# Projections of two gated cross-attention layers as three float32r products

## The reference, cut to what matters

```python
def layer(x, ctx, attend, ffn, g):        # two layers, B=4, S=512, D=256, 16 heads of 16
    x = x + tanh(g_xattn) * attend(norm(x), ctx, ctx)
    return x + tanh(g_ffn) * ffn(norm(x))
# layer 0: Q = x@Wq.T + bq, K = ctx@Wk.T + bk, V = ctx@Wv.T + bv
#          softmax(Q K / 4 - 0.1*|i-j|) V, then @Wo.T + bo; FFN with ternary weights (256-1024-256, relu)
# layer 1: relu(x@Wq.T), relu(ctx@Wk.T), relu(ctx@Wv.T), softmax attention without bias
#          FFN with 4 experts, argmax routing (256-1024-256, gelu), then a layer norm of its own
```

## Time and profile before

| | us |
|---|---|
| median of 3 runs (766.58 to 767.68) | 766.68 |
| the profiled execution | 764.96 |
| its span | 763.1 |

### The profile page before, as it was taken

One profiled execution on the slowest core, in us unless ns is written; L12 is line 12 of the kernel. 1 busy time (PEld: TensorE's weight loads), 2 busy tenths in 40 slices (PEclk: granted clock), 3 DMA queues, 4 the chain that ended last, 5 costly groups with the idle time before them and its releaser, 6 DMA issues.

```text
span 763.1 us, 12507 instructions
## 1 busy us (share of the span) xinstructions
PE 702.1 (92%) x4252; PEld 424.1 (56%) x4252; DVE 565.4 (74%) x1054; ACT 451.5 (59%) x968; POOL 340.8 (45%) x409
## 2 busy tenths in 40 slices
PE   6878999999998898899998999999999699999993
PEld 3444444444443566597763444444444488989983
DVE  5565899999992369455887999999996656765663
ACT  2322788888888443765414888888887234333330
POOL 3213455555555232763520021645653555755542
PEclk9999999999999999999999999999999889999998
DMA  7788645554554514102144255422201222211000
GB/s 222 214 263 187 200 144 182 180 188 144 182 191 170 166 55 114 40 1 78 37 123 112 79 180 177 140 85 84 76 3 74 85 109 78 78 36 51 27 15 15
DMA packets 51421, 87.53 MB, mean 115 GB/s; under 512 B 8661, under 2 KB 16855, under 8 KB 51360
## 3 DMA queue, kind: packets, MB, share of 16 engines
q1 hardware_dynamic: 43184, 71.39, 29.7%
q0 software_dynamic: 4640, 11.54, 5.1%
q10 hardware_dynamic: 3536, 3.81, 1.7%
HBM read 44.92 MB, written 41.63 MB: 113 GB/s over the span
## 4 chain that ended last, share of the span: by engine, by line
PE 58%; DVE 13%; POOL 12%; issue 8%; DMA 4%; SPq 3%; ACT 2%; POOLq 0%; DVEq 0%; ACTq 0%
PE ps_out L811 9%; PE ps_out L1029 6%; PE ps_wide L1004 6%; PE ps_wide L680 6%; PE ps_a L794 6%; PE ps_a L596 4%; PE ps_misc L794 3%; PE ps_a L929 3%; POOL w_lo L1312 3%; SPq L495 2%; PE ps_a L1018 2%; DVE rows_all L1559 2%; PE ps_out L943 2%; PE ps_wide L607 1%; DMA rows_all<-in_x 1%
## 5 line engine op out<-in xcount | busy, mean ns | idle before, releaser
L1593 DVE TENSOR_REDUCE row_max<-ps_wide 128x2 f32<-128x1024 f32 x256 | 301.9, 1220 | 20.4 <-PE ps_wide L680 19.6
L1142 ACT ACTIVATE probs<-ps_a 128x512 f32<-128x512 f32 (+1 forms) x418 | 199.1, 522 | 28.3 <-PE ps_a L794 27.7
L680 PE MATMUL ps_wide<-stack_k,stack_q 48*128 48x512 f32 x512 | 145.1, 469 | 7.9 <-DVE row_max L1593 3.9
L794 PE MATMUL ps_a<-stack_q,stack_k 62*128 62x512 f32 (+3 forms) x418 | 137.5, 391 | 2.9 <-ACT probs L1142 1.9
L811 PE MATMUL ps_out<-probs,vals 128*17 128x512 f32 x1024 | 134.1, 598 | 0.5 <-POOL probs L1372 0.5
L1142 ACT ACTIVATE probs<-ps_misc 128x512 f32<-128x512 f32 (+1 forms) x222 | 114.0, 514 | 16.4 <-PE ps_misc L794 13.8
L1372 POOL TENSOR_TENSOR probs<-probs,fixes_sb 128x512 f32<-128x512 f32 x64 | 82.2, 1285 | 90.3 <-ACT probs L1142 90.3
L794 PEld LDWEIGHTS ps_a<-stack_q,stack_k 62*128 62x128 f32 (+1 forms) x418 | 63.6, 184 | 68.3 <-ACT probs L1142 31.5
L680 PEld LDWEIGHTS ps_wide<-stack_k,stack_q 48*128 48x128 f32 x512 | 68.3, 184 | 46.9 <-DVE row_max L1593 27.0
L794 PE MATMUL ps_misc<-stack_q,stack_k 62*128 62x512 f32 (+3 forms) x222 | 87.7, 395 | 1.3 <-ACT probs L1142 1.3
L794 PEld LDWEIGHTS ps_misc<-stack_q,stack_k 62*128 62x128 f32 (+1 forms) x222 | 40.9, 184 | 39.1 <-ACT probs L1142 30.4
(11 more groups left out here) (246 smaller groups left out, 1341.1 us busy)
## 6 DMA issues: line engine op xcount, KB each, us to landing
rows_sorted<-blank SPq DMA_DIRECT2D x17, 1040.0 KB, 5.0
planes_k<-planes SPq DMA_DIRECT2D x32, 256.0 KB, 3.7
stack_k<-planes_k SPq DMA_DIRECT2D x64, 128.0 KB, 2.8
planes_q<-planes SPq DMA_DIRECT2D x32, 256.0 KB, 3.6
stack_q<-planes_q SPq DMA_DIRECT2D x64, 128.0 KB, 2.8
w_raw<-in_L_W SPq DMA_DIRECT2D x6, 1024.0 KB, 5.8
stack_k<-planes_k SPq DMA_DIRECT2D x64, 64.0 KB, 2.5
stack_q<-planes_q SPq DMA_DIRECT2D x64, 64.0 KB, 2.7
```

Of the source, the lines that this page charges most:

```text
L680: mm(raw_slot(l, ("pair", g, p))[:, i * S:(i + 1) * S], stack_q[at, slot(g, c) + q * P:slot(g, c) + (q + 1) * P], stack_k[at, slot(g, c):s ...
L794: mm(score_slot(("tile", n))[:, start:end], stack_k[at, slot(g, c) + k * P:slot(g, c) + (k + 1) * P], stack_q[at, slot(g, c) + start:slot( ...
L1142: do(probs[n % PROBS[l]][:, j, start:end], score_slot(("tile", n * TILES + t))[:, start:end], ACT.Exp, scale=0.25).then_inc(exp_done, 1)
L1593: v.tensor_reduce(row_max[:, g % 2, :, p], raw_slot(l, ("pair", g, p))[:].rearrange("p (i k) -> p i k", i=2), AX, ALU.max).then_inc(sem(f" ...
```

## The change

Keys, values and queries of both layers are made as three products of float32r parts (high by high, low weights by high rows, high weights by low rows) instead of float32 matmuls: six matmuls a unit, twelve a values step. The context is split once into `ctx_hi` and `ctx_lo` and used by both layers: batch 0 by ScalarE (high) and VectorE (low), batches 1 to 3 by GpSimd (`context_split(b + 1)` behind `keys_low(0, b)`). Layer 0's weights are split by VectorE (w_k, and every low part) and ScalarE (high parts of w_v and w_q); layer 1's by GpSimd (`weights_split`: w_k at group 4 of layer 0's attention, w_v behind that attention, w_q behind layer 1's keys). Turned rows get a high part from ScalarE's copy and a low part from VectorE (`rows_low0`, `rows_low2`), for which queries and the reuse of the banks now wait. `xT` is gone; the attention's output goes to `att_rows`. ScalarE runs one small copy at the very start. In the experts' stage `prepare(3)` moves ahead of the roots of blocks 0 and 1, and `finish` scales the rows before it waits for the root. Several semaphores are shared between the two layers (counts go on from l * G); those lines are left out.

```diff
+                ctx_lo = sb("ctx_lo", [P, C, B * S], F32R, inputs_)
+            turned_x = sb("turned_x", [P, 2, C, S], F32R, pro)
...
+                att_rows = sb("att_rows", [P, 2, C, S], F32, s0)
+                sb("gap_stacks", [P, 2 * RING * S], F32, s0)
+                w_v_hi1 = sb("w_v_hi1", [P, C, D], F32R, s0)
...
+                x_parts = [sb(f"x_{h}", [P, 2, C, S], F32R, s1) for h in PARTS]
+                w_v_hi0 = sb("w_v_hi0", [P, C, D], F32R, s1)
+                w_q_hi0 = sb("w_q_hi0", [P, C, D], F32R, s1)
...
+        def context_parts(b):
+            return ctx_hi[:, :, b * S:(b + 1) * S], ctx_lo[:, :, b * S:(b + 1) * S]
+
+        def rows_parts(b):
+            return [part_[:, b % 2] for part_ in x_parts]
+
+        def weight_parts(l, s_):
+            hi = {(0, "k"): w_k_hi, (0, "v"): w_v_hi0, (0, "q"): w_q_hi0, (1, "k"): w_k_hi, (1, "v"): w_v_hi1, (1, "q"): w_k_hi}[l, s_]
+            return hi[:], w_lo[s_][:]
 
         def turned_of(b):
-            return turned_x[:, b % 2]
+            return turned_x[:, 0], turned_x[:, 1]
...
-                for k in range(C):
-                    last = mm(proj_bank(l, s_, b, c), w_qkv[s_][:, k, c * P:(c + 1) * P],
-                              src(b)[:, k], start=(k == 0), stop=(k == C - 1))
+                weights, rows = weight_parts(l, s_), src(b)
+                for i, (r, w) in enumerate(PRODUCTS):
+                    if i == 0 and (l, s_, b) == (0, "k", 0):
+                        pe.wait_ge(sem("parts_high"), C)
+                        pe.wait_ge(sem("parts_low"), 2)
+                    if i == 2 and (l, s_, b) == (0, "k", 0):
+                        pe.wait_ge(sem("parts_low"), 2 + C)
+                    if i == 0 and (l, s_, b) == (0, "q", 0):
+                        pe.wait_ge(sem("parts_low"), C + 4)
+                    if i == 2 and (l, s_) == (0, "q"):
+                        pe.wait_ge(sem("x_low"), C * (b + 1))
+                    if i == 0 and l == 0 and s_ == "k" and b > 0:
+                        pe.wait_ge(sem("ctx_low"), C * b)
+                    if i == 0 and (l, s_, b) == (1, "q", 0):
+                        pe.wait_ge(sem("ctx_low"), C * (B - 1) + 3)
+                    if (l, s_) == (1, "q") and i == (0 if b == 0 else 2):
+                        pe.wait_ge(sem("x_low"), C * (B + b + 1))
+                    if i == 0 and (l, s_, b) == (1, "k", 0):
+                        pe.wait_ge(sem("ctx_low"), C * (B - 1) + 1)
+                    for k in range(C):
+                        last = mm(proj_bank(l, s_, b, c), weights[w][:, k, c * P:(c + 1) * P], rows[r][:, k],
+                                  start=(i == 0 and k == 0), stop=(i == 2 and k == C - 1))
                 last.then_inc(made(l, s_, "proj_done", b, c)[0], 1)
...
+                if v == 0 and l == 0:
+                    pe.wait_ge(sem("parts_low"), C + 3)
+                elif v == 0:
+                    pe.wait_ge(sem("ctx_low"), C * (B - 1) + 2)
+                weights, rows = weight_parts(l, "v"), context_parts(v // 2)
                 for i in range(2):
-                    t = 2 * v + i
-                    for k in range(C):
-                        last = mm(vals_bank(l, v)[:, i * D:(i + 1) * D], ctxT[:, k, t * P:(t + 1) * P], w_qkv["v"][:, k, :],
-                                  start=(k == 0), stop=(k == C - 1))
+                    at = slice((2 * v + i) % QT * P, ((2 * v + i) % QT + 1) * P)
+                    for n, (r, w) in enumerate(PRODUCTS):
+                        for k in range(C):
+                            last = mm(vals_bank(l, v)[:, i * D:(i + 1) * D], rows[r][:, k, at], weights[w][:, k, :],
+                                      start=(n == 0 and k == 0), stop=(n == 2 and k == C - 1))
...
-                        pe.wait_ge(sem("turned_read_n2"), (b - 1) * C + c + 1)
+                        pe.wait_ge(sem("x_low"), (B + b - 1) * C + c + 1)
...
-                    wait(pe, sem("turned_read_n0"), (b - 1) * C + i + 1)
+                    wait(pe, sem("x_low"), (b - 1) * C + i + 1)
...
-                        last = mm((po, pm)[t % 2][:, 0:D], xT[:, k, t * P:(t + 1) * P], w_o[:, k, :],
+                        last = mm((po, pm)[t % 2][:, 0:D], att_rows[:, b % 2, k, t % QT * P:(t % QT + 1) * P], w_o[:, k, :],
...
+                    if name == "n0":
+                        do(x_parts[0][:, b % 2, c, :], spare_banks[c][:], ACT.Copy).then_inc(sem("turned_read_n0"), 1)
+                    else:
+                        do(att_rows[:, b % 2, c, :], wide(u), ACT.Copy).then_inc(sem("turned_read_att"), 1)
...
+            act.wait_ge(sem("half_ready"), 1)
+            do(quant[:, 0:1], minus_half[:, 0:1], ACT.Copy)
...
+            for c in range(C):
+                do(ctx_hi[:, c, 0:S], context_of(0)[:, c, :], ACT.Copy).then_inc(sem("parts_high"), 1)
...
+                    if b == 0:
+                        act.wait_ge(loaded_values, 16 * N_VALUES)
+                        do((w_v_hi0, w_q_hi0)[c][:], w_qkv["vq"[c]][:], ACT.Copy).then_inc(sem("parts_high"), 1)
...
+            def context_split(b):
+
+                pool.wait_ge(sem(f"loaded_in{b}"), 16 * N_IN)
+                for c in range(C):
+                    hi, lo, raw = (z[:, c, b * S:(b + 1) * S] for z in (ctx_hi, ctx_lo, ctxT))
+                    v.tensor_copy(hi, raw).then_inc(sem("ctx_high"), 1)
+                    pool.wait_ge(sem("ctx_high"), C * (b - 1) + c + 1)
+                    v.tensor_tensor(lo, raw, hi.bitcast(F32), ALU.subtract).then_inc(sem("ctx_low"), 1)
...
+            def weights_split(s_):
+
+                n = C * (B - 1) + "kvq".index(s_) + 1
+                (hi, lo), raw = weight_parts(1, s_), w_qkv[s_][:]
+                pool.wait_ge(sem("w_layer1"), 16 * 3)
+                v.tensor_copy(hi, raw).then_inc(sem("ctx_high"), 1)
+                pool.wait_ge(sem("ctx_high"), n)
+                v.tensor_tensor(lo, raw, hi.bitcast(F32), ALU.subtract).then_inc(sem("ctx_low"), 1)
...
+                    if l == 0 and g == QT:
+                        weights_split("k")
...
                 keys_low(0, b)
+                if b + 1 < B:
+                    context_split(b + 1)
...
             attention(0)
+            weights_split("v")
             for b in range(B):
                 keys_low(1, b)
                 roots(1, b)
+            weights_split("q")
...
                 gather(FIRST + n)
+            prepare(3)
             for n in range(2):
                 root4(n)
             for n in range(2):
                 scatter(n)
             for n in range(2, BLOCKS):
                 root4(n)
-                if n + 1 < BLOCKS:
+                if 2 < n < BLOCKS - 1:
                     prepare(n + 1)
...
+            def weight_low(s_):
+
+                hi, lo = weight_parts(0, s_)
+                v.tensor_tensor(lo, w_qkv[s_][:], hi.bitcast(F32), ALU.subtract).then_inc(sem("parts_low"), 1)
+
+            def rows_low0(b):
+
+                for c in range(C):
+                    dve.wait_ge(sem("turned_read_n0"), b * C + c + 1)
+                    v.tensor_tensor(x_parts[1][:, b % 2, c, :], spare_banks[c][:], x_parts[0][:, b % 2, c, :].bitcast(F32), ALU.subtract
+                                    ).then_inc(sem("x_low"), 1)
+
+            v.tensor_copy(w_k_hi[:], w_qkv["k"][:]).then_inc(sem("parts_low"), 1)
+            dve.wait_ge(sem("parts_low"), 1)
+            weight_low("k")
+            for c in range(C):
+                dve.wait_ge(sem("parts_high"), c + 1)
+                v.tensor_tensor(context_parts(0)[1][:, c, :], context_of(0)[:, c, :], ctx_hi[:, c, 0:S].bitcast(F32), ALU.subtract
+                                ).then_inc(sem("parts_low"), 1)
             dve.wait_ge(loaded_rows, 16 * N_ROWS)
             variance(0, 0, x, 1e-5)
+            dve.wait_ge(loaded_values, 16 * N_VALUES)
+            dve.wait_ge(sem("parts_high"), C + 1)
+            weight_low("v")
             normal(0, 0, x)
-            dve.wait_ge(loaded_values, 16 * N_VALUES)
+            dve.wait_ge(sem("parts_high"), C + 2)
+            weight_low("q")
             for b in range(B):
                 for c in range(C):
                     first_maxima(0, *FIRST_RAWS.get((b, "k", c), (0, 0)))
                 for i in range(2):
                     values0(2 * b + i)
                     first_maxima(0, *FIRST_RAWS.get((b, "v", i), (0, 0)))
+                rows_low0(b)
...
                 if b == B - 1:
-                    dve.wait_ge(sem("turned_read_n0"), B * C)
+                    dve.wait_ge(sem("x_low"), B * C)
...
+            def rows_low2(b):
+
+                for c in range(C):
+                    dve.wait_ge(sem("turned_read_n2"), b * C + c + 1)
+                    v.tensor_tensor(turned_x[:, 1, c], n2_bank(b, c), turned_x[:, 0, c].bitcast(F32), ALU.subtract
+                                    ).then_inc(sem("x_low"), 1)
...
                     if q == 1 and b == 1:
+                        rows_low2(0)
```

(11 more changed lines are left out.)

58 lines of the change are left out of this document (31 added, 27 removed).

## The result

The changed kernel takes 773.64 us (median of 5, 770.57 to 775.74) against 766.58 us (763.51 to 767.68) for the kernel before: a ratio of 1.0103, 95% interval 1.0078 to 1.0128. It is slower, by 7 to 8 us where the forecast had 2.3 and a range up to 772.5. The profiled execution is the fastest of its five, 770.57 us with a span of 768.2; against the profiled one of before (763.1) it is 5.1 us longer.

The account below looks back on a forecast made before the run. TensorE holds 58% of the chain but does not end the first stage, where VectorE and GpSimd do. First stage +5.7, third -1.9 and experts -1.5 sum to +2.3 us: forecast 769.0 us, range 762.5 to 772.5.

Parts of the forecast that it names:

- The signs that the forecast named: Batch 1 keys near 29.5, attention 5.7 us later, clock fall before 50, shorter third stage, `turned_x` low wait, no 1.8 wait.
- The saving on TensorE: Projections: 0.32 us saved per key or query unit, 0.31 per values step; 15.2 us in all, as a ceiling.
- The head: First stage, first batch: splitting and GpSimd beside VectorE delay keys of batch 1 by 6.6 us, to 29.5; low end 2.7.
- Rival 1: Head is cheaper: first batch loses only 2.7 us, batch 1 keys at 25.6, total 763.7 us; chance 0.27.
- Batches 1 to 3: First stage after the head: +0.5, -0.8 and -2.0 us for batches 1, 2 and 3.
- The clock: First stage: of two 3.7 us TensorE pauses, one is followed by a clock fall costing about 1.4 us.
- the third (771.4): Rival: clock falls twice in the first stage and again beside the wait of query batch 1; 771.4 us, chance 0.13.
- Layer 0's attention: The w_k split on GpSimd, 1.9 us once, is covered by idle time: 0; without cover 1.9 us.
- Third stage, keys and values: Layer 1's keys and values save 5.1 us, less 1.3 where VectorE is last and 0.6 for GpSimd: -3.2 us.
- Third stage, the rest: Layer 1's queries wait for low parts, +1.3 us in sum; whole third stage -1.9 us, bounds -4.5 and +0.5.
- Experts: Last stage: moving `prepare(3)` and scaling earlier gives 1.1 us, last block's scaling 0.4; -1.5 us, bounds -0.4 and -2.2.

Follow-up runs that it names:

- split_later: Changed kernel with GpSimd's context split of batch 1 held until VectorE has made the low part of the query weights; ratio 1.0111 to the kernel before.
- all_filled: queries_first plus unread matmuls in three third-stage gaps, GpSimd's batch 1 split held back, and 6 unread matmuls before batch 0's turning; ratio 0.9969 to the kernel before.
- fillers: Changed kernel with unread matmuls in TensorE's first-stage gaps (12 before batch 0's turning, 14 behind the queries of batches 1 and 2); ratio 1.0137 to the kernel before.
- queries_first: Changed kernel with VectorE making the queries' low halves of a batch ahead of the next batch's normal rows in the first stage; ratio 1.0020 to the kernel before.
- stats_first: Changed kernel with VectorE's statistics of the next batch ahead of the low parts of this batch's turned rows; ratio 1.0089 to the kernel before.
- all_three: Changed kernel with the edits of split_later, stats_first and fillers together; ratio 1.0107 to the kernel before.
- layer0_f32: Changed kernel with layer 0's keys, values and queries in float32 and GpSimd's context splits in groups 0 to 3 of its attention; ratio 1.0166 to the kernel before.

## Why the prediction was wrong

The direction was right, and so was the bound: TensorE does not end the first stage. The size was off by 5 us of 7. Of the 4.6 us between 769.0 and 773.64, 2.5 are the first stage, 0.4 layer 0's attention, 1.1 the third stage and -1.2 the experts, all by the two profiles; 0.5 lie outside the span, and 1.4 are that the median stands 3.1 us above the profiled execution where the forecast allowed 1.7. The signs that the forecast named all came (the third stage up to the first up-projection is 3.2 us shorter, TensorE waits 1.97 us for the low part of `turned_x`); it is sizes that failed, and for layer 1 by the runs the sign. Step by step:

**The saving on TensorE.** Right. 2.97 us for two units (forecast 2.80), 1.41 for a values step (1.42).

**The head.** Right in size and mechanism: +6.0 us at the keys of batch 1 (forecast 6.6, at 28.87 instead of 29.5). `w_v_lo` took 1.28 us, the four normal rows 4.05 beside GpSimd's low plane and split. Rival 1 (25.6) fell. The Trainium skill (SBUF — State Buffer, SBUF: two separate sides) has a shared pair of ports that either GpSimd or a VectorE operation in a two-port mode, or with two SBUF inputs, holds for a whole instruction; split_later agrees, since with the split moved the four rows took 2.44 us and the head was 1.5 us shorter. What the forecast didn't see is that this term isn't additive: in all_filled keys of batch 1 come 3.9 us earlier and the last weighing doesn't.

**Batches 1 to 3: the step that failed.** The forecast had +0.5, -0.8 and -2.0 for the three batches and 1.4 for one fall of the clock, -0.9 in all. Measured are +0.7, +1.4 and +0.1, the clock included: +2.2.

- Batch 1 was right: the forecast's own 2.0 for `rows_low0` less 1.3 for keys and values is 0.7. Keys and values count there, since turning, low parts and statistics stand behind them. The queries' saving does not: VectorE goes on for 3.62 us after they are done.
- Batch 2: the keys ran at half clock, 4.56 us instead of 2.97, and these 1.6 us are on the chain (split_later and fillers show the price). The rows' landing did not end last any more, as forecast, but the low parts and statistics that stand behind the values now did (53.34 and 54.53), so that the rest is -0.2 instead of -0.8.
- Batch 3 is the largest miss, 2.1 us. Both key units ran at half clock, so that from their start to ScalarE's `full` it is 5.7 us (63.53 to 69.27) against 5.9 before (55.40 to 61.28): 0.1 saved, not 1.0. The values' 0.6 came to nothing, because GpSimd's maxima end last there: TensorE waits 1.67 us for them, and from `full` to its return at 75.41 it is 6.14 us against 6.11 before. The first query saved its 0.3. At the end TensorE starts 0.66 us behind VectorE's last plane, before 0.11; the cause of that 0.5 is open.

So the failed step is what the forecast took back in batches 2 and 3, 2.8 us: it was counted where VectorE or GpSimd ended last, and at a clock that the new gaps took away. The forecast also took VectorE's order as given. Having the normal rows in front of the queries' low halves is what queries_first takes off, 6 us with the falls behind the gaps.

**The clock.** The forecast took one fall of 1.4 us. The profile shows four in the first stage (near 20, 44, 60 and 84 us), and they don't cost alike. The first made the first queries 5.37 us instead of 3.04 and cost nothing, for TensorE then waited 1.31 us all the same; the second cost 1.6. With them the first stage is +8.2 instead of +5.7. Of the three rivals the third (771.4) was nearest.

**Layer 0's attention.** 0.4 instead of 0.

**Third stage, keys and values.** Right: -3.7 against -3.2 (8.7 at its start, 5.0 at the first up-projection), and VectorE was last between batches 2 and 3; its normal rows took 1.38 there, not 3.31, but two small steps ahead of them 1.25 and 1.20, so that nothing was won by it.

**Third stage, the rest.** The queries came as worked out (+1.3, -0.5, +1.6 and -0.5, together +1.9 against +1.3). Missing was 1.0 us in GpSimd's eight low halves of the hidden layer (13.1 us together, 12.05 before, of which the earlier trace rows shows the first 7.08); what held them up was not tried. Total of the profile -0.8, forecast -1.9. And missing was the larger thing: the shorter products leave TensorE gaps of 3.0, 2.5 and 2.0 us, behind which most profiles with layer 1's products show the clock halved (split_later, stats_first, all_three and queries_first have all three falls). The profiled execution of the changed kernel has gaps of 3.06 and 1.97 us at the first and third place, the second in two pieces (1.40 and 1.61), and none of the falls. Its other four executions are 2.0 to 5.2 us longer, at a mean clock of 0.972 to 0.976 against its 0.978. That they lost it in the third stage is inferred from the edited kernels, not seen. By the runs this term changed its sign.

**Experts.** Right: -1.4 for `prepare(3)` and -0.3 for the scaling (forecast -1.1 and -0.4). The wait of 1.81 us is 0.44 now:

```profile
653.55 0.73 PE L1051 MATMUL ps_wide<-w_hi,sortedT_lo 128*128 x2 [0.44 <-DVE sortedT_lo L2012]
```

Another 1.4 us of the difference of the two profiles is luck with the clock ahead of the first expert block (+8.2 us at 618, +6.7 behind it): before had the clock at 0.66 and 0.50 in the slices from 608 and 612, after at 0.72 and 0.85 in those from 616 and 620.

The sum by the runs: layer 0 +8 to +10, layer 1 about +3, experts -3, each to some 2 or 3 us; 8 to 10 together, beside the measured 7.9 (1.0103).

## What to carry to other kernels

Before a saving on one engine is counted, ask of each wait that follows whose chain ends it, and follow that chain back: here keys and values stood on VectorE's chain and their saving counted, the queries did not. Where the engine is off the chain the saving is nothing, and what the change adds to the other engine's queue counts in full. When operations are added to an in-order engine, look at what stands behind them that somebody else waits for, and put that first: here this was worth 6 us, where each change to the head alone moved the ratio by 0.0008 or less. Read the granted clock in more than one profile, because a gap that costs nothing in one was followed by a fall worth about 1.5 us in another.

## What the hardware showed that was not expected

Behind the same gap the clock is halved in one profile and not in another. Ahead of the last output projections TensorE idled 3.06 us in the changed kernel, and the next slices were at 1.00; it idled 3.03 us in queries_first, and the next was at 0.64. The changed kernel's timeline:

```profile
304.00:308.00 4.00, 2.77 (x17) 2.44 (x18) 3.86 (x11) 0.24 (x1) 0.00 (x0) 1.00 0.69 214
```

The Trainium skill (TensorE: Matmul & The Clock Gate, Part 1: The HAM clock gate) says that the unit which watches TensorE runs free of the kernel's own start, so that one kernel fares differently from run to run. The two profiles agree with that, though they are of two kernels.

A lower mean clock isn't a longer time by itself. The mean over all runs was 0.975 for the changed kernel and 0.976 for queries_first, 6 us faster; and in the changed kernel the fall near 20 us cost nothing, that near 44 us 1.6. Here a fall cost only where TensorE was on the chain.

GpSimd's cover in attention is thinner than its idle time suggests: 90.3 us of idle before 64 fixes hid 1.9 us in one group for 0.4, but 3.7 us in each of four groups made them 14.2 us long (102.23, 116.49 and 130.68 in the chain of layer0_f32), where layer 0's attention of before has 10.8. Part of this can be the halved clock behind the new waits; the two were not told apart.
